# A second norm computed from moments, tile weights on ScalarE, and taps summed in PSUM

## What is computed

```python
x = x + L0(groupnorm32(x))   # dilated dynamic convolution, then a batch norm of its output y
x = x + (codebook[argmin_j |z - c_j|^2] - z),  z = groupnorm32(x)   # 8192 codes, L1
x = x + depthwise3x3(groupnorm32(x), kern = relu(pooled @ Wk.T + bk))   # L2
x = x + L3(groupnorm32(x))   # two deformable 3x3 convolutions, each with group norm and relu
```

## Time and profile before

| what | value |
|---|---|
| median of 3 executions | 1700.38 us (1697.67 to 1702.74) |
| profiled execution: its own time | 1702.24 us |
| profiled execution: span from first to last instruction | 1700.4 us |
| mean granted clock of TensorE | 0.891 of full speed |
| busy: PE, DVE, POOL, ACT | 1312.0, 1156.8, 999.7, 416.2 us |
| first to last row of the norm between | 318.22 to 345.38 us |
| first search matmul | 346.85 us |
| end of the search on VectorE | 848 us |
| first gather of tile 5, of tile 10 | 903.46, 973.83 us |

### The profile page before, as it was taken

The page is one execution under the profiler, slowest core; times in us unless marked ns, Lnnn a source line. Parts: engine busy times, 40 slices in busy tenths (PEclk is TensorE's granted clock), DMA queues, the critical chain, the costliest instruction groups (busy, mean ns, idle before and its releaser), DMA issues.

```text
span 1700.4 us, 22882 instructions
## 1 busy us (share of the span) xinstructions
PE 1312.0 (77%) x7855; PEld 913.7 (54%) x7898; DVE 1156.8 (68%) x1477; ACT 416.2 (24%) x1287; POOL 999.7 (59%) x979
## 2 busy tenths in 40 slices
PE   5888999488998888679855599687667867676675
PEld 2345555244444444334435578666567666666675
DVE  4667678679999999998966947544455444554444
ACT  2241000213343432333431132222112212121111
POOL 4256568222344442325776877777777777777772
PEclk9889999789999999889976799799898989877877
DMA  4041000011111111133474597787777878776773
GB/s 151 25 161 39 2 0 0 0 45 38 45 32 57 57 52 30 32 104 113 133 232 131 163 291 240 212 247 246 232 226 210 266 229 248 209 233 211 210 210 115
DMA packets 111112, 232.84 MB, mean 137 GB/s; under 512 B 14676, under 2 KB 60500, under 8 KB 110748
## 3 DMA queue, kind: packets, MB, share of 16 engines
q0 software_dynamic: 58176, 191.30, 37.4%
q1 hardware_dynamic: 52828, 40.17, 7.5%
HBM read 205.15 MB, written 26.26 MB: 136 GB/s over the span
## 4 chain that ended last, share of the span: by engine, by line
POOL 29%; PE 23%; issue 16%; DVE 11%; ACT 1%; DMA 0%; another core or an unknown queue 0%; POOLq 0%; DVEq 0%; ACTq 0%
POOL code_region L1843 11%; POOL max_region L1843 6%; POOL early_region L1843 5%; POOL late_region L1843 5%; PE score L1249 5%; PE score L1250 5%; PE score L1248 5%; DVE max_region L1650 3%; PE score L1271 3%; DVE x L267 2%; PE turn_ps L1152 1%; PE turn_ps L1280 1%; DVE code_region L1686 1%; PE score L1182 1%; DVE n_stats L152 1%
## 5 line engine op out<-in xcount | busy, mean ns | idle before, releaser
L1650 DVE SCALAR_TENSOR_TENSOR max_region<-score,nc,max_region 128x512 f32<-128x512 f32 x504 | 347.6, 740 | 37.5 <-PE score L1250 35.2
L1843 POOL DMA_INDIRECT code_region<-corners,lead_region x252 | 251.9, 999 | 76.6 <-issue 75.4
L1686 DVE TENSOR_TENSOR code_region<-score,code_region 128x4608 f32<-128x4608 f32 x28 | 138.8, 4957 | 125.2 <-DMA code_region<-corners,lead_region 124.9
L675 POOL TENSOR_TENSOR prod_acc<-prod_acc,prod_pool 128x752 f32<-128x752 f32 (+8 forms) x112 | 149.0, 1330 | 107.0 <-DVE prod_pool L648 99.6
L1271 PE MATMUL score<-ident,code_region 128*128 128x128 f32 x1008 | 146.0, 316 | 56.5 <-DVE code_region L1686 56.5
L1271 PEld LDWEIGHTS score<-ident,code_region 128*128 128x128 f32 x1008 | 140.3, 167 | 61.1 <-DVE code_region L1686 59.8
L1843 POOL DMA_INDIRECT early_region<-corners,lead_region x136 | 133.1, 979 | 41.3 <-issue 40.8
L1443 ACT COPY code_region<-score 128x384 f32<-128x384 f32 x144 | 68.8, 479 | 361.6 <-PE score L1271 361.5
L1843 POOL DMA_INDIRECT max_region<-corners,lead_region x130 | 123.4, 949 | 39.6 <-issue 39.3
L1843 POOL DMA_INDIRECT late_region<-corners,lead_region x126 | 119.4, 948 | 43.7 <-issue 37.8
L1761 POOL DMA_INDIRECT late_region<-code_rows,block_id x35 | 37.8, 1081 | 157.6 <-DVE block_id L1497 99.0
(11 more groups left out here) (210 smaller groups left out, 2561.8 us busy)
## 6 DMA issues: line engine op xcount, KB each, us to landing
corners<-lead_region SPq DMA_DIRECT2D x72, 192.0 KB, 4.4
corners<-lead_region SPq DMA_DIRECT2D x8, 576.0 KB, 7.1
code_rows<-codes_n SPq DMA_DIRECT2D x8, 516.0 KB, 4.2
codes_t<-in_codes_t SPq DMA_DIRECT2D x8, 512.0 KB, 3.6
codes_n<-in_codes SPq DMA_DIRECT2D x8, 512.0 KB, 4.5
code_region<-corners,lead_region POOLq DMA_INDIRECT x252, 3.7
x<-in_x SPq DMA_DIRECT2D x2, 1152.0 KB, 6.6
out<-x SPq DMA_DIRECT2D x4, 576.0 KB, 3.2
```

Of the source, the lines that this page charges most:

```text
L675: pool.tensor_tensor(to, to, v, ALU.add).then_inc(pooled, 1)
L1650: dve.scalar_tensor_tensor(r, score[SLOT[k]][:], nc2[:, m:m + 1], r, ALU.add, ALU.max).then_inc(dve_took, 1)
L1686: dve.tensor_tensor(q4, bc(wps[:, u * n:(u + 1) * n], P), q4, ALU.mult).then_inc(weighted, 1)
L1843: pool.indirect_dma_start(quad(T, k), None, table[j].rearrange("n s c -> n (s c)"), bass.IndirectOffsetOnAxis(index[j % B][:, at:at + 1], 0))\
```

## The change

There are five parts.

1. The block of the norm between is gone. Its work is a class `Between`, at the start of `finale`. In the branches VectorE additionally sums `x*y` over each 768 columns. From the moments of the input, of `y` and this sum, the moments of `x + s*y + t` follow on single columns. Only the first 512 columns are normed by VectorE and ScalarE; GpSimd makes all the rest of `x` and `z` beside chunk 0 of the search, and the others wait for that (`between.rest`) before chunk 1.
2. ScalarE multiplies tiles 2, 3 and 4 by their corner weights, 36 activations of 128 columns each (`product`), tile 2's ahead of its copies for tile 1, those of tiles 3 and 4 between its copies of the tile before.
3. Image 1's taps are done in halves of 1152 columns, whose running sum lies in three PSUM banks; only the first tap reads `x` and only the last writes it.
4. Tile 2 takes the place of tile 1 in the pieces apart and tile 1 a slot; GpSimd gathers tile 6 ahead of tile 5. Tile 1 moves on TensorE and ScalarE ahead of image 1's norm.
5. For the last chunk VectorE forms the code numbers (`name_code`), with no GpSimd instruction between its DMAs.

```diff
-def norm_between(nc, tools, x, y, stats, gb, gm32, norm, z, zh, zl):
...
+    def half_tap(self, dve, b, h, k, sums):
...
+        dve.scalar_tensor_tensor(sums if k < TAPS - 1 else xb, v, self.kern[:, k:k + 1], sums if k else xb,
+                                 ALU.mult, ALU.add).then_inc(self.done[b], 1)
...
+                        dve.scalar_tensor_tensor(xy_each[:], y[:, bass.ds(at, 2 * CH)], 1.0,
+                                                 x_flat[:, bass.ds(at, 2 * CH)], ALU.mult, ALU.mult,
+                                                 accum_out=xy[:, bass.ds(b * CHUNKS + o["q"] - 1, 1)])
...
+        chain(dve.scalar_tensor_tensor(first, self.y[:, 0:self.FIRST], s, first, ALU.mult, ALU.add))
...
+        chain(dve.tensor_scalar(z, first, scale[:, 0:1], self.first_shift[:, 0:1], ALU.mult, ALU.add))
+        dve.wait_ge(self.high, 1)
+        dve.tensor_tensor(zl, z, zh, ALU.subtract).then_inc(self.low, 1)
...
+        pool.tensor_scalar(x[:, 0:self.FIRST], x[:, 0:self.FIRST], self.t[:], None, ALU.add).then_inc(rest, 1)
+        v = slice(self.FIRST, N)
+        pool.tensor_scalar(y[:, v], y[:, v], self.s[:], self.t[:], ALU.mult, ALU.add).then_inc(rest, 1)
+        pool.wait_ge(rest, 2)
+        pool.tensor_tensor(x[:, v], x[:, v], y[:, v], ALU.add).then_inc(rest, 1)
...
-                    pe.wait_ge(z1_ready, 6)
+                    pe.wait_ge(between.rest, between.DONE)
...
+        tap_sums = sums_ps[:, 0:HW // 2]
...
+            def product(T, g):
+                act.wait_ge(landed(T), quads_of(T))
+                for k in range(3 * g, 3 * g + 3):
+                    for c in range(CORNERS):
+                        v, at = quad(T, k)[:, c * P:(c + 1) * P], (T * TAPS + k) * CORNERS + c
+                        act.activation(v, v, ACT.Identity, scale=weights[0][:, at:at + 1]).then_inc(act_weighted, 1)
...
+                    if T + 1 in BY_SCALAR[1:]:
+                        product(T + 1, g)
...
-                for t in range(TAPS):
-                    if t % 3 == 0:
-                        T = 2 + t // 3
-                        tile(0, T // TPC, T % TPC)
-                    if t == 3:
+                for t in range(2 * TAPS):
+                    if t == TAPS:
                         weigh(0, 2, 4)
-                    depthwise.tap(dve, 1, t)
+                    depthwise.half_tap(dve, 1, t // TAPS, t % TAPS, tap_sums)
...
-                    apart.wait_ge(turn_done, 3 * TPC + 3 * (T - SLOTS if T > SLOTS + 1 else 0) + 3)
+                    apart.wait_ge(turn_done, 3 * TPC + 3 * (T - SLOTS if T > SLOTS + 2 else T - SLOTS - 1) + 3)
...
+                rows(6)
                 apart.wait_ge(x_added, 1 + 2 * NPX)
-                for T in range(5, ITILES):
+                rows(5)
+                for T in range(7, ITILES):
                     rows(T)
```

More of the change, by code:

```diff
@@ L303, in _ @@
                 norm.dve_affine(dve, b, ps[:])
+                dve.tensor_copy(moments[:, b, :], norm.mv[:])
         @block.tensor
@@ L916, in finale @@
     M = ITILES * TAPS
+    APART = 2
+    BY_SCALAR = 2, 3, 4
     LEAD_STORES = 2
@@ L1318, in _ @@
             pe.sem_inc(mixed, 3)
+            between.pe(pe, gps[:, 0:2 * B])
             search_steps(step)
@@ L1395, in step @@
                 if S == STEPS:
-                    act.wait_ge(z1_ready, 6)
+                    act.wait_ge(between.rest, between.DONE)
                 if S >= 2:
@@ L1458, in first_job @@
                 tile(0, 0, 0)
+                act.wait_ge(wps_ready, 1)
+                for g in range(3):
+                    product(BY_SCALAR[0], g)
+                tile(0, 0, 1)
                 depthwise.act_norm(act, 1)
-                for T in range(1, 5):
+                for T in range(2, 5):
                     tile(0, T // TPC, T % TPC)
@@ L1640, in step @@
                 if S == STEPS:
-                    dve.wait_ge(z1_ready, 6)
+                    dve.wait_ge(between.rest, between.DONE)
                 for k in range(BY_ACT, NPR):
```

322 lines of the change are left out of this document (192 added, 130 removed).

## The result

The changed kernel takes 1676.4 us (median of 4 runs, 1673.2 to 1679.3) against 1700.4 us (4 runs, 1697.7 to 1702.7): a ratio of 0.986, 95% interval 0.9841 to 0.9879. The forecast was 1669.6 us, range 1662 to 1682. A later series on a chip where the kernel before takes the same time gave 1675.3 against 1699.7 us, 0.9858 (0.9838 to 0.9878). The difference of the medians is 24.0 and 24.4 us, forecast 30.8. The profiled execution of the changed kernel took 1679.3 us, with a span of 1677.5 us, 22.9 under the span before.

What follows compares the result with a forecast made beforehand. GpSimd's gathers set the end, so earlier gains reach it one for one unless a later wait takes them. Norm -16.5, branches +2.0 and tile 10's earlier start -16.3 sum to -30.8: 1669.6 us, range 1662 to 1682.

Steps and rivals of the forecast that it cites:

- The price in the branches: Branch loop: four added products of x and y, 0.95 us each, delay partly passed on; 2.0 us lost, bounds 0 and 3.8.
- Image 0's last statistics: Behind the branch loop, in VectorE's 4.95 us of idle time: cost nothing; without that cover 2.0 us.
- rival C: Ahead of tile 10: tile 5 is turned before GpSimd finishes tile 9, so tile 10 starts at 950; 1662 us, chance 0.05.
- The norm: Between the layers: first row to first search matmul in 12.1 us instead of 28.6, 16.5 us earlier, bounds 13 to 17.5.
- The fetches: Last codes ahead of the first job: four bare DMAs 1.25 us apart, the last fetch 5.9 us earlier.
- Part 4 ahead of the taps: Image 1's norm start, behind tile 1 on TensorE and ScalarE: group matmul at 903.4, taps' kernel ready at 910.9, 2.9 us earlier.
- Parts 2 and 3: First job: half taps of 1.44 us, ScalarE's products 0.30 apart and hidden, 28.7 us to the norm's statistics, 15.7 earlier.
- The gap ahead of tile 10: GpSimd idles 5 to 9 us, ended by TensorE's turning of tile 5; tile 10 starts 16.3 us earlier, no later gap.
- A: First job: ScalarE is late at 0.40 us per product, tile 10 at 963.4, 10.4 us gained; 1675.5 us, chance 0.13.
- D: Image 1's taps: PSUM write and read back make a half tap 3.6 us, tile 10 at 996; 1708 us, chance 0.04.
- B: Beside the taps: gathers stay stretched, 14 us stay on GpSimd's queue, tile 10 near 964; 1676 us, chance 0.11.

Runs made afterwards that it cites:

- the second pair: Both kernels profiled again, unedited, on chips that run the kernel before in 1700 us: before 1698.1 us (one run), changed 1675.3 us, ratio 0.9858.
- the four traces: Two profiles each of the unedited kernel before and changed kernel; first search matmul 28.6 and 28.2 us behind the norm's first row before, 12.6 and 12.2 changed.
- the two experiments on the taps: Changed kernel with image 1's nine full taps, sum in SBUF: 1936.9 us, ratio 0.9976 (slower chip); with 18 half taps, sum in SBUF: 1681.8 us (one run).

## Why the forecast came out 7 us too good

The direction and all mechanisms but one were right, and 1676.4 us lies in the range. What failed is a size.

**The price in the branches is the term that was mis-sized.** The step read: "four more products over 768 columns in the loop, 0.95 each", "a delay passes on in part", "Bounds 0 and 3.8; I take half, 2.0 lost". It measured 4.7 us (218.1 less 213.4, both without low stretches but the one around 135 us), above its own upper bound. Two things were wrong in it. The duration came from operations that read one operand from PSUM; two of the four products meet an addition of GpSimd and last 1.53 us. And the half that passes on came from TensorE's total of waits over the whole loop, which says nothing on one place; the window around it shows VectorE busy in all of 5.00 us. Image 0's last statistics, "in VectorE's 4.95 us of idle time", were free to 0.3 us: from the last tap product to the norm's first row 5.3 us went by before and 5.6 after. The bounds of the terms alone give 1665.5 at the lower end; the 1662 of the range is rival C's time.

**The clock was not in the sum.** Low stretches cost the first profiled execution of the changed kernel 5.4 us more than that of before, and in the second pair it was the other way round by 1.9 us (219.8 less 217.0 is 2.8, of which 4.7 are the products). A forecast made against one execution carries that; the range had no term for it. With the products' extra 2.7 us, 0.5 us in the norm's chain and 0.1 to 1.9 us more in the search and the fetches (their cause is open), 3.3 to 5.1 of the 6.4 to 6.8 us that the medians fell short are named; the rest is within what single executions differ by (1670.0 to 1679.3 us for the changed kernel).

**The norm** was right: 12.2 and 12.6 us for 12.1. It was not undone by itself; its verdict rests on the four traces. `between.rest` on GpSimd took 31 us from 340.76 on, 29.3 forecast, and nothing waited for it.

**The fetches** are 1.25 us apart. Counted from the first search matmul the last comes 5.8 and 4.0 us earlier, for 5.9, though the search in that leg got 1.2 and 1.1 us longer.

**Part 4 ahead of the taps**: the group matmul came 7.2 us behind the start of image 1's moments, 6.3 forecast, the first half tap 7.0 behind the matmul, 7.5 forecast.

**Parts 2 and 3**: 28.9 us from the first half tap to the statistics, 28.7 forecast; half taps of 1.45 for 1.44; ScalarE's products at 0.30 for 0.30. The gap ahead of tile 10 was 5.6 us, in the 5 to 9 named, and none behind. What part 4's new order of tiles 5 and 6 is worth by itself isn't shown.

**The rivals**: A (0.40 per product of ScalarE) and D (3.6 us per half tap) fall by those rows. B falls by the two experiments on the taps. C, the closed gap at 1662, needed an earlier tile 5, for which the forecast saw no row; moving its product ahead of the norm closes it, and then the next wait shows. That this kernel took 1663.4 us, near C's 1662, is chance: the closed gap gave 1.4 us of it.

## What to carry to other kernels

An operation added to a saturated stretch costs its whole length there; read the window around the place, not the engine's sum of waits, and look for a wait of the same engine to put it in. When a wait is closed, look at once for the next one on the same queue: here 5.0 us were bought ahead of tile 10 and 3.6 given back ahead of tile 11. Take a second profile of the same kernel before explaining a few us by the clock.

## What the hardware showed

A gather on GpSimd's queue that begins during a VectorE operation with two SBUF inputs ends 0.8 us behind the end of that operation (1.15 us long beside 1.45 us half taps, 2.35 beside 2.65 us taps, 0.95 where one input lies in PSUM, also when the output goes to SBUF). A VectorE operation with two SBUF inputs that starts during an addition of GpSimd ends 0.8 us behind it (1.54 for 0.94 us). The same share of work of TensorE, 3.27 of 5 us busy, went with a granted clock of 0.87 and then 0.78 in one execution and of 1.00 in another.
